# Attention stage: maxima of eight units turned at once, first scores nine units ahead

## What is computed

```
x = x + attention(layernorm(x))      # x: 8 batch elements x 256 tokens x 128
qkv = x @ w_qkv.T + b_qkv            # 16 heads of 8 dimensions
att = q @ k.T / sqrt(8) + bias       # bias from positions, per head
att = softmax(causal(att))           # 256 x 256 for each head
out = (att @ v) @ w_proj.T + b_proj
```

## Time and profile before

| | us |
|---|---|
| median of 3 runs (lowest, highest) | 1195.49 (1194.45, 1196.18) |
| the profiled execution's own time | 1195.5 |
| its span, first to last instruction | 1193.8 |
| TensorE busy in the span | 1026.2 (86%) |
| VectorE, ScalarE, GpSimd busy | 943.2, 781.3, 802.9 |
| mean granted TensorE clock | 0.919 |
| first score of attention starts | 936.73 |

### The profile page before, as it was taken

The page is one execution under the profiler, slowest core; times in us unless marked ns, Lnnn a source line. Parts: engine busy times, 40 slices in busy tenths (PEclk is TensorE's granted clock), DMA queues, the critical chain, the costliest instruction groups (busy, mean ns, idle before and its releaser), DMA issues. The chain is left out here.

```text
span 1193.8 us, 21258 instructions
## 1 busy us (share of the span) xinstructions
PE 1026.2 (86%) x7673; PEld 529.2 (44%) x7673; DVE 943.2 (79%) x1737; ACT 781.3 (65%) x1722; POOL 802.9 (67%) x449
## 2 busy tenths in 40 slices
PE   5799999999899999999999999883485799999465
PEld 2344444444444444444444444341254466666244
DVE  3578888888988889888898898996795346664895
ACT  4868888787787878878878778851242145554342
POOL 1488988879798798898997988993343023322252
PEclk8899998999999999999999999997687579999688
DMA  6544334435344435444444343403600100000001
GB/s 231 168 153 127 146 122 143 125 115 169 109 148 129 135 124 164 123 141 127 143 132 138 124 144 127 146 32 81 99 1 0 18 19 17 5 19 2 0 1 36
DMA packets 65403, 118.89 MB, mean 100 GB/s; under 512 B 40004, under 2 KB 46980, under 8 KB 56324
## 3 DMA queue, kind: packets, MB, share of 16 engines
q1 hardware_dynamic: 65300, 117.54, 31.3%
HBM read 109.13 MB, written 6.29 MB: 97 GB/s over the span
## 5 line engine op out<-in xcount | busy, mean ns | idle before, releaser
L838 POOL TENSOR_TENSOR prod<-hid,c_rep 128x1024 f32<-128x1024 f32 x256 | 605.0, 2391 | 117.1 <-DVE hid L774 117.1
L774 DVE TENSOR_TENSOR_SCAN hid<-decay,acc 128x256 f32<-128x256 f32 x1024 | 606.7, 662 | 69.2 <-PE acc L497 67.2
L676 ACT ACTIVATE decay<-delta,a_neg 128x255 f32<-128x255 f32 x1024 | 423.3, 497 | 14.3 <-DVE hid L774 14.1
L497 PE MATMUL acc<-b_diag,du_t 64*128 64x256 f32 x2048 | 294.3, 407 | 24.2 <-DVE hid L774 24.2
L497 PEld LDWEIGHTS acc<-b_diag,du_t 64*128 64x128 f32 x2048 | 179.0, 188 | 201.7 <-issue 116.6
L511 PE MATMUL ring<-prod,ident 64*64 64x512 f32 x2048 | 261.9, 629 | 4.1 <-POOL prod L838 3.4
L1663 POOL TENSOR_SCALAR_AFFINE_SELECT att_probs<-att_probs 128x512 f32<-128x512 f32 x64 | 40.6, 634 | 133.5 <-ACT att_probs L1707 133.5
L511 PEld LDWEIGHTS ring<-prod,ident 64*64 64x64 f32 x2048 | 68.7, 138 | 126.9 <-issue 118.7
L1707 ACT ACTIVATE att_probs<-acc 128x384 f32<-128x384 f32 x128 | 55.8, 488 | 79.1 <-PE acc L1474 79.1
L414 PE MATMUL ring<-xpad,diag_cw 64*64 64x512 f32 x512 | 62.1, 601 | 0.9 <-ACT xpad L593 0.9
L1472 PE MATMUL acc<-att_qk 17*128 17x256 f32 x256 | 56.7, 461 | 0.5 <-ACT att_probs L1707 0.4
(11 more groups left out here) (165 smaller groups left out, 1374.1 us busy)
## 6 DMA issues: line engine op xcount, KB each, us to landing
c_rep<-c_rows SPq DMA_DIRECT2D x64, 1024.0 KB, 4.8
b_diag<-diag_rows SPq DMA_DIRECT2D x64, 512.0 KB, 3.8
diag_rows<-prod SPq DMA_DIRECT2D x2, 2048.0 KB, 10.8
att_qk<-in_pos_q SPq DMA_DIRECT2D x4, 768.0 KB
att_qk<-att_dense SPq DMA_DIRECT2D x32, 64.0 KB
att_qk<-in_pos_k SPq DMA_DIRECT2D x4, 288.0 KB
resid<-in_x SPq DMA_DIRECT2D x4, 256.0 KB, 3.1
c_rows<-bc SPq DMA_DIRECT2D x64, 8.0 KB, 1.4
```

The source lines that it names most:

```text
L497: last = nc.tensor.matmul(inj[:, K % 2, at:at + HALF * SG], du_t[rows, n % 2, e, q * INNER + h * P:q * INNER + (h + 1) * P], b_diag[rows, ...
L676: last = nc.scalar.activation(decay[:, K % DECAYS, s, 1:], delta[:, n % 2, h, e * SEQ + 1:(e + 1) * SEQ], ACT.Exp, scale=a_neg[:, lay(n) % ...
L774: last = nc.vector.tensor_tensor_scan(hid[:, K % HIDS, s, :], decay[:, K % DECAYS, s, :], rows[:, s, :], 0.0, ALU.mult, ALU.add)
L838: nc.gpsimd.tensor_tensor(prod[:, K // 4 % 2, h, :, at], hid[:, K % HIDS, :, :], c_rep[:, g, :, at], ALU.mult).then_inc(s_prod, 1)
```

## The change

The maxima of all eight units of a batch element are transposed once. In each strip, head group g writes its maxima to row 16 + g, and only that head group's keys hold ones in that row (zeros in the other three), so all four rows can be added to the queries of all four head groups by one addition of 128x1024 with a broadcast. The transposes and the addition come once in eight steps, 8 times in all. All first scores of a batch element must be done by then, so S_LEAD becomes 9: steps -9 to -1 have first scores alone, steps 55 to 63 turned scores alone. Chunks 0 and 1 are projected ahead of the loop (EARLY = 3), chunk 2 in steps -8 to -5, chunk 3 in steps 2, 6, 8 and 9. Queries and keys of these first three chunks use the banks `t0` and `t1`. `dense` gets two buffers, with a semaphore each.

```
-S_LEAD, PV_LAG, TURN_LAG, OUT_LAG = 3, 3, 4, 12
+S_LEAD, PV_LAG, TURN_LAG, OUT_LAG = 9, 3, 4, 12
+EARLY = 3
...
-        self.use("a", "x", 0), self.use("t0", "q", 0), self.use("t1", "k", 0), self.use("v", "v", 0)
+        for c in range(EARLY - 1):
+            self.use("a", "x", c), self.use("t0", "q", c), self.use("t1", "k", c), self.use("v", "v", c)
...
+                q, k = ("t0", "t1") if n < EARLY else ("a", "a")
...
     if u % 2:
-        piece("peak", (u + 1) // 2, GROUPS)
+        if (u + 1) % 8 == 0:
+            piece("peak", (u + 1) // 8, BATCH)
...
-        if 0 <= u and u % per == 9:
-            piece("v", u // per + 1, CHUNKS)
+        if u >= 0 and u % per == 9:
+            piece("v", u // per + EARLY, CHUNKS)
...
-            if 0 <= u and u % per == when:
-                piece(kind, u // per + 1, CHUNKS)
+            if u >= 0 and u % per == when:
+                piece(kind, u // per + EARLY, CHUNKS)
+    if -S_LEAD < u <= 4 - S_LEAD:
+        piece("xqkv"[u + S_LEAD - 1], EARLY - 1, CHUNKS)
...
-        dense = sb("dense", [P, 2, CH])
+        dense = sb("dense", [P, 2, 2, CH])
...
-        s_strip = sem("att_strips_loaded")
+        s_strip = [sem(f"att_strips_{n}_loaded") for n in ("even", "odd")]
...
-            return slice(j * STRIP, j * STRIP + MAX_ROW + 1)
+            return slice(j * STRIP, j * STRIP + MAX_ROW + HGROUPS)
...
-                        t.wait_ge(s_strip, 2 * STRIPS * 16 * (s // per + 1))
+                        c = s // per
+                        t.wait_ge(s_strip[c % 2], 2 * STRIPS * 16 * (c // 2 + 1))
...
-                        banks.wait_read(t, "peak", u // 2)
+                        banks.wait_read(t, "peak", u // 8)
...
-                def turn_peaks(g):
-                    banks.wait_free(t, "peak", g)
-                    banks.wait_read(t, "s", 2 * g)
-                    banks.wait_read(t, "s", 2 * g + 1)
+                def turn_peaks(b):
+                    banks.wait_free(t, "peak", b)
+                    banks.wait_read(t, "s", 8 * b + 6)
+                    banks.wait_read(t, "s", 8 * b + 7)
...
-                turn_x(0)
-                project(0, 0)
-                project(1, 0)
-                project_v(0)
+                for c in range(EARLY - 1):
+                    turn_x(c)
+                    project(0, c)
+                    project(1, c)
+                    project_v(c)
...
-                def add_row(g):
-                    b, hg = g // HGROUPS, g % HGROUPS
-                    banks.wait_filled(v, "peak", g)
-                    q = qk[:, 0, b // CH_BATCH, hg, b % CH_BATCH, :]
-                    banks.read(nc.vector.tensor_tensor(q, q, banks.bank("peak", g)[:, 0:SEQ], ALU.add), "peak", g)
+                def add_rows(b):
+
+                    banks.wait_filled(v, "peak", b)
+                    q = qk[:, 0, b // CH_BATCH, :, b % CH_BATCH, :]
+                    rows = banks.bank("peak", b)[:, 0:SEQ].unsqueeze(1).broadcast_to([P, HGROUPS, SEQ])
+                    banks.read(nc.vector.tensor_tensor(q, q, rows, ALU.add), "peak", b)
...
-        pos[1, j, HD, g] = 1.0
+        pos[1, j, HD + g, g] = 1.0
```

More of the change, by code:

```diff
@@ L1490, in both_scores @@
                                 score_turned(u, i, 1 - tile)
-                def turn_peaks(g):
-                    banks.wait_free(t, "peak", g)
-                    banks.wait_read(t, "s", 2 * g)
-                    banks.wait_read(t, "s", 2 * g + 1)
+                def turn_peaks(b):
+                    banks.wait_free(t, "peak", b)
+                    banks.wait_read(t, "s", 8 * b + 6)
+                    banks.wait_read(t, "s", 8 * b + 7)
                     for c in range(2):
-                        last = nc.tensor.transpose(banks.bank("peak", g)[:, c * P:(c + 1) * P], npk[:, g % 2, c, :], ident[:, :])
-                    banks.fill(last, "peak", g)
+                        last = nc.tensor.transpose(banks.bank("peak", b)[:, c * P:(c + 1) * P], npk[:, b % 2, c, :], ident[:, :])
+                    banks.fill(last, "peak", b)
                 def mix(g):
@@ L1630, in _ @@
                 normalise(0)
+                for c in range(1, EARLY):
+                    moments(c)
+                normalise(1)
                 tiles.wait(v)
                 values(0)
+                for c in range(2, EARLY):
+                    normalise(c)
+                for c in range(1, EARLY - 1):
+                    values(c)
                 v.wait_ge(s_npk, 1)
@@ L1635, in _ @@
                     work = iteration(u)
+                    ahead = u // per + EARLY
                     for kind, n in work:
                         if kind == "peak":
-                            add_row(n)
-                    if 0 <= u and u % per == 2 and u // per + 1 < CHUNKS:
-                        normalise(u // per + 1)
+                            add_rows(n)
+                    if 0 <= u and u % per == 2 and ahead < CHUNKS:
+                        normalise(ahead)
                     for kind, n in work:
@@ L1650, in _ @@
                             values(n)
-                    if 0 <= u and u % per == 0 and u // per + 1 < CHUNKS:
-                        moments(u // per + 1)
+                    if 0 <= u and u % per == 0 and ahead < CHUNKS:
+                        moments(ahead)
             @block.gpsimd
@@ L1674, in _ @@
                 nc.gpsimd.tensor_copy(mask_b[:, :, :], tiles.mask[:, :].unsqueeze(1).broadcast_to([P, 2, P])).then_inc(s_maskb, 1)
-                out_bias(0)
+                for c in range(EARLY):
+                    out_bias(c)
                 for u in range(UNITS):
                     causal(u)
-                    if u % per == 3 and u // per + 1 < CHUNKS:
-                        out_bias(u // per + 1)
+                    if u % per == 3 and u // per + EARLY < CHUNKS:
+                        out_bias(u // per + EARLY)
             @block.scalar
@@ L1697, in add_bias @@
                     banks.wait_filled(a, kind, c)
-                    need(a, s_strip, 2 * STRIPS * 16 * c)
-                    banks.read(nc.scalar.activation(dense[:, m, :], banks.bank(kind, c), ACT.Identity, bias=tiles.bqk[:, m:m + 1]), kind, c)
+                    need(a, s_strip[c % 2], 2 * STRIPS * 16 * (c // 2))
+                    banks.read(nc.scalar.activation(dense[:, c % 2, m, :], banks.bank(kind, c), ACT.Identity, bias=tiles.bqk[:, m:m + 1]), kind, c)
                 def exps(u):
@@ L1724, in _ @@
                 copy_x(0)
+                rstd(1)
                 tiles.wait(a)
@@ L1727, in _ @@
                 add_bias(1, 0)
+                for c in range(2, EARLY):
+                    rstd(c)
+                for c in range(1, EARLY - 1):
+                    copy_x(c)
+                    add_bias(0, c)
+                    add_bias(1, c)
                 for u in ITERATIONS:
@@ L1730, in _ @@
                         exps(u)
-                    if 0 <= u and u % per == 1 and u // per + 1 < CHUNKS:
-                        rstd(u // per + 1)
+                    if 0 <= u and u % per == 1 and u // per + EARLY < CHUNKS:
+                        rstd(u // per + EARLY)
                     for kind, n in iteration(u):
```

16 lines of the change are left out of this document (8 added, 8 removed).

## The result

| | before | changed |
|---|---|---|
| median of 4 runs, us | 1195.50 | 1211.0 (1208.0 to 1215.47) |
| ratio, 95% interval | | 1.0134 [1.0097, 1.017] |
| profiled execution, own time (span) | 1195.5 (1193.8) | 1213.04 (1211.3) |
| mean granted clock | 0.919 | 0.899 |

A second series on another chip gave 1208.26 against 1197.63, ratio 1.0092 [1.0057, 1.0127]. The change makes the kernel slower by about 1%; 1208.6 had been forecast.

The account below looks back on a forecast made before the run. TensorE was taken to bound the attention stage, its work priced at the granted clock. Terms -9.2 + 2.9 + 12.7 + 6.0 - 4.7 + 5.4 = +13.1 on 1195.5 gave 1208.6 us, 8-in-10 range 1199 to 1216.

Parts of the forecast that it names:

- six more lead units: Before the first turned scores: six units of first scores alone, 2.11 us each at half clock, +12.7 us.
- chunk 2 in the lead: In the lead: chunk 2's transposes and three projections have nothing beside them, +6.0 us at half clock.
- units 0 to 8: First joint steps: three transposes of maxima fewer, 0.48 us each at half clock; TensorE stands about 0.3 us per later addition.
- six more units at the end: Stage's end: turned scores alone, clock falling early, one pair at full clock and 3.5 at half, +5.4 us with the last mixing.
- start to the first score: Gap before the first score: chunk 1's projections fit into the 8.1 us idle time, cost 0.
- TensorE sets the pace: Whole attention stage: TensorE limits it, and its work counts double at 1.2 GHz of what it counts at 2.4 GHz.
- rival 4: Whole stage: the transposes were not on the path, so only the costs remain, 1218 us; chance 0.03.
- The addition of 128x1024: After each batch element's transposes: 1.20 us on VectorE, TensorE waiting for it, +2.9 us in all; upper end 1.69 us each.
- rival 3: Gap and first units: late start, late clock rise or 1.69 us addition, each +2 to +4, 1211 to 1216 us; chance 0.12.
- some 19: Sign of being right: first turned score near 963 to 964 us, some 19 us later than before.
- rival 1: Lead: the clock rises at chunk 2's projections and stays up, sum -6.0, 1189.5 us; chance 0.13.
- Rival 2: Stage's end: the clock holds through it, so 6.4 us of cost goes, 1202 us; chance 0.14.

Follow-up runs that it names:

- e1: Changed kernel run again with no edit, on another chip: 1208.3 us, stage 202.1 us.
- e2_groups: Changed kernel with transposes and additions back to one for each head group and eight buffers of maxima: 1219.0 us, stage 210.2 us.
- e3: Changed kernel plus unread products: 12 of 128x384 in the gap before the first score, one ahead of each lead unit: 1210.3 us, stage 198.9 us.
- e5: Changed kernel plus unread products, re-measured: six in the gap, small ones in steps up to 6 and at the end: 1187.8 us, ratio to before 0.9938.
- e9: Changed kernel plus two unread products ahead of each of the nine turned-only steps at the end, none elsewhere: 1209.2 us, stage 197.2 us.
- e8: Kernel before with chunk 1 projected in the gap, plus unread products in gap, early steps and end: 1183.2 us, ratio 0.9901.
- e6: Kernel before plus unread products: 12 in the gap, small ones in steps up to 6 and the last three: 1185.7 us, ratio 0.991.
- e10: Changed kernel with transposes once a head group and a lead of five units in place of nine: 1195.3 us (one run), stage 195.4 us.
- e4: Kernel before plus unread products: 22 in the gap before the first score, one ahead of each of three lead units: 1200.4 us, stage 192.4 us.

## Why the prediction was right, point by point

The stage's pieces against the sum's terms, in the profiled execution:

| term | forecast | measured |
|---|---|---|
| six more lead units | +12.7 | +12.7 (2.12 each) |
| chunk 2 in the lead | +6.0 | +6.5 (0.91 and 3 x 1.87) |
| first addition | +0.8 | +0.9 |
| units 0 to 8: three transposes at half clock less, one stand | -1.4 + 0.3 = -1.1 | -2.7 |
| units 8 to 56: transposes, stands, two chunks | 18 x 0.37 less, 6 x 0.3 and -4.7: -9.6 | -9.6 |
| six more units at the end, three transposes less | +5.4 - 3 x 0.37 = +4.3 | +6.3 (5.6 and 0.7); in e1 +4.2 |
| start to the first score | 0 | +0.5 |
| sum | +13.1 | +14.6 |

The three terms of the lead make 20.1 and are what the lead's column shows (29.4 - 9.2).

- **TensorE sets the pace**: right. e2_groups gives back the transposes at their price, and the eight-unit period came out at 16.76 for the 16.8 worked out. That settles rival 4. That a microsecond of TensorE work counts double at the lower clock is a little too much by the prediction's own rows: a lead unit is priced at 2.11 for 1.18 and a pair of transposes 0.48 for 0.37. TensorE was also not quite "never idle" up to 970: it stood 0.38 us at 951.71.
- **The addition of 128x1024** takes 1.22 us, as its nearest row had it, not the 1.69 of the addition from SBUF, and TensorE stands 2.7 us for it in all, where the sum had 2.9. Of rival 3 only a start 0.5 us late came true.
- **The lead runs at the lower clock, and chunk 2's projections don't lift it**: right in the profiles of both chips. The first turned scores came 21.7 us later than before (965.99, before 944.3) for the "some 19" named as a sign. The doubt was real: with products that nothing reads in the gap and among the same units the clock stays up in the lead (e3, e5), and a lead unit then takes 1.17 us (935.24 to 936.41 in e5) for the 1.18 of rival 1.
- **The clock falls early at the end**: right, within the first two of the nine turned-only units (in e1 to e3 3.6 us after the exponentials of unit 56). e9 shows it as the cause of the loss there. The pair took 5.64 us for the 5.4 estimated.
- **Two terms were mis-sized**, in opposite directions. Units 0 to 8 got 2.7 us shorter and not 1.1. Of that, 2.1 came in steps 0 to 5, with the clock at 0.50 in both kernels. Counted from one unit's exponentials to the next one's, the three steps that lost their transposes got 0.62 to 0.66 us shorter, where the sum took 0.48 for a pair, as it costs in the lead; among the joint steps of before a pair takes 0.61 from start to start (954.75 to 955.36, below). Step 2, where the chunk's transposes had stood behind an idle time of 0.38 us, got 0.2 shorter. Another 0.9 (0.7 in e1) came in step 6, since the clock rose sooner after the start of the chunk's first projection: after 1.6 us (985.79 to 987.4), in before after 3.6 (966.17 to 969.8). The stand for the addition in step 7 took its 0.3 back. In the ten profiles in which the clock was low there, the rise came 1.6 to 3.6 us after that start; what sets it within that range is open. The end cost 6.3 and not 4.3: the sum had the clock hold for a pair, and it held for less; when it fell later (e1) the end was at 4.2. The forecast of no cost ahead of the first score missed 0.5 us.
- **What was luck**: the mechanisms held, but that the sum of 13.1 lies within 1.5 us of the 14.6 owes something to the two misses (-1.6 and +2.0) cancelling. The medians moved by 15.5 us on the first chip and by 10.6 on the second.
- **Rival 1** did not come by itself. Its number can be held against e5: it gave a stage of 189.3 - 6.0 = 183.3. e5 took 179.8 but also held the end, worth 6.8 in e9; without that it is 186.6, with the filling's own cost in it. So the mechanism is shown, its size roughly. **Rival 2** (clock holds at the end) was priced at 6.4 us; forced by e9 it saved 6.8 of the stage (4.9 against e1).

The pair of transposes at half clock among the joint steps, in the kernel before:

```profile
954.75 0.69 PE L1497 MATMUL acc<-ident,att_npk 128*128 128x128 f32 x2
955.36 1.04 PE L1513 MATMUL acc<-att_probs,att_v 128*9 128x256 f32 x8
```

What of the change is worth keeping? With the clock held in both, the changed kernel's stage (e5, 179.8) is 4.6 us longer than that of the kernel with a lead of three and one chunk in the gap (e8, 175.2): the lead costs 12.7 more (six units, chunk 2 and the addition), units 0 to 56 give 7.3 back (2.3 of it is chunk 2, which is not in them), the end 0.8. With the chunks left alone the difference would be smaller: an estimate for e6 with its clock held is 175.2 + 2.3 = 177.5, 2.3 less than the 179.8 of e5, and the medians of e5 and e6 differ by 2.1, which can't be told from nothing. Turning maxima once a batch element is a gain (6.2 us, e2), but the lead of nine that it asks for costs more than it brings. That holds for this order of steps; a lead that has turned scores of another batch element beside it was not tried.

## What to carry to other kernels

When a step is put further ahead, count the units that lose their partner at both ends: each lead unit stands alone once at the start and once at the end, here 2.0 us a unit at the start and 1.4 at the end (e10: 7.9 and 5.6 for four), which no saving of 6 us in all pays for. Price each piece at the clock that is granted where it will run, and look in the trace for which work held the clock and which did not; thin products kept TensorE busy without a break and still ran at half clock. If such a stretch can't be avoided, a few products that nothing reads may pay: they made the changed kernel's stage some 22 us shorter, and with one chunk moved into the gap the kernel before 1% faster. Too many in the wrong place cost what they gain (e3, e4).

## What was not expected of the hardware

- What makes the clock fall among thin work is open. Stands of 1.09 us (e3) and 1.11 us (e6) came ahead of a fall that lasted 20 and 17 us. But in e4 it fell with one stand of 0.30 us ahead of it and no filling in the joint steps, and in e8 it held through a stand of 1.11 us at the same step as in e6, with the same filling in the steps. Nor was it tested whether the products in the gap or the small ones in the steps hold it in the lead; only both together were tried.
- Queries with 20 rows cost what 17 cost: a lead unit took 2.12 us, before 2.11.
- On the chip of e1 to e4 the stage's start lay anywhere from 914.3 to 923.0 us in the profiled executions, with the same stages ahead of it (911.8 to 924.5 over all of e1 to e10), and the kernel before ran from 1191 to 1208. The two stages of the changed kernel that were profiled differ by 1.9 us. So pieces of a stage can tell a difference that the totals blur, though each is read from one execution.
